# Second attention: stacks of single heads in half the partitions

## The chip, the cores and the metric

One core of one Trainium2 chip runs the whole program. The metric is the device time of one execution in microseconds (us); the median of several runs counts. TensorE (PE) multiplies, VectorE (DVE), ScalarE (ACT) and GpSimd (POOL) work on what it leaves, and SyncE (SP) issues nearly all transfers.

## What is computed

A two-layer network in float32 over 2 x 512 tokens of width 512. Each layer is attention and a feed-forward part, each followed by a residual sum and a layer norm. The change lies in the second attention: 32 query heads of 16 columns, 8 key/value heads, so that four query heads share one key head, causal.

```python
B, T, D_IN, D_OUT = (2, 256, 512, 512)
N_HEADS, N_KV = (32, 8)
HEAD_DIM = D_OUT // N_HEADS
...
q = _apply_rope(q, cos, sin)
k = _apply_rope(k, cos, sin)
k_h = jnp.repeat(k, GROUP_SIZE, axis=1)
v_h = jnp.repeat(v, GROUP_SIZE, axis=1)
scores = jnp.einsum('bhqd,bhkd->bhqk', q, k_h) / math.sqrt(HEAD_DIM)
causal = jnp.triu(jnp.ones((t, t), dtype=bool), k=1)
scores = jnp.where(causal[None, None], jnp.finfo(scores.dtype).min, scores)
attn = jax.nn.softmax(scores, axis=-1)
ctx = jnp.einsum('bhqk,bhkd->bhqd', attn, v_h)
```

(The sizes in the first line are not used: the arrays passed in have T = 512.)

## The kernel before

The program runs first attention, first feed-forward, second attention and second feed-forward one after another, each engine with an instruction list written out by hand. Products use a split of each float32 operand in a high and a low part (`fp32r`): `three` at L92 adds high x high, high x low and low x high.

In the second attention (`attention1`, L1253) a *unit* u is one key head of one batch (16 units), with four query heads; a *slot* s is one query head (64 slots). A head has only 16 columns, so the three terms of the split don't need three products: they are laid one under another in the partitions and one product sums over all. These layouts are the *stacks*. Before the change a stack holds a pair of heads: `q_stack` has the rows [q_hi; q_hi; q_lo] of two heads (3 x 32 = 96 partitions) for two pairs, and `k_stack` has two versions of [k_hi; k_lo; k_hi], each with the rows of the other head left at zero. Four stacks of each kind go round (`STACKS`, L1217). Turned queries and keys lie in `qT_hi`, `qT_lo`, `kT_hi`, `kT_lo`, and SP copies their rows into the stacks by transfers within the on-chip memory.

A slot does this. `scores` (L1911) computes the scores with queries in the partitions, four tiles of rows in three PSUM banks; VectorE takes each row's maximum (`maxima`, L1709). This runs seven slots ahead (`LEAD`). Once the four heads of a unit are through, PE turns the maxima (`turn_tops`, L1947), ScalarE copies them negated (`copy_tops`, L1514), and SP writes them as further rows of the query stack (`load_tops`, L1456), where the key stack has ones. `key_scores` (L1932) then computes the scores again, keys in the partitions and the maximum already taken off (98 rows), ScalarE takes exponentials (`exps`, L1506), GpSimd clears the masked triangles (`prune`), and `apply` (L1960) multiplies by the values, four heads at once in four column tiles of the array; from slot 5 on, three slots of four carry one of its three parts (L1978). `turn_output` (L1985) turns a unit's output, in the first slot of a unit.

The order of PE's slot, scores of s + 7 and keys of s alternating by bank (L2079):

```python
for s in range(SLOTS1):
    for piece in range(PIECES):
        if s + LEAD < SLOTS1:
            scores(s + LEAD, piece)
        key_scores(s, piece)
    if s % GROUP1 == 1 and s + 3 < SLOTS1:
        turn_tops((s + 3) // GROUP1)
```

SP's order, in one queue: stacks of units 0 and 1, then for every unit u the maxima of u (waiting for `top_ready`), then the stacks of u + 2 (waiting for `keyed` of unit u - 2, whose buffers they take). The score products of unit u + 2 start in slot 4u + 1 and wait for `stack_in`.

GpSimd prepares the key stacks (`pad_keys`, L1625: a fill with zeros and a select that writes the ones) between its additions for the rotation.

Of the kernel before, what the change touches and what calls it, by code (L numbers as in the profile page):

```python
# [10 lines left out]
F32 = mybir.dt.float32  # L11
# [4 lines left out]
P = 128  # L16
# [1177 lines left out]
PARTS = 3  # L1194
PAIR_ROWS = 2 * HD1
STACK = PARTS * PAIR_ROWS
# [19 lines left out]
STACK_DMAS = 16 * (2 * PARTS + 2 * PARTS)  # L1216
STACKS = 4  # L1217
TOP_ROW = STACK
STACK_ROWS = STACK + 2
# [33 lines left out]
def attention1(nc, t, w_o, w_f1, lora_b_in, small_in, result, psum):  # L1253

    ctx = ExitStack()
    with ctx:
# [17 lines left out]
        q_stack = [sb(f"q_stack{n}", [P, 2, SEQ], F32R) for n in range(2)]  # L1274
        k_stack = [sb(f"k_stack{n}", [P, 2, SEQ], F32R) for n in range(2)]
# [19 lines left out]
        q_stack.append(sb("q_stack2", [P, 2, SEQ], F32R))  # L1295
        k_stack.append(sb("k_stack2", [P, 2, SEQ], F32R))
# [6 lines left out]
        q_stack.append(over("q_stack3", [P, 2, SEQ], b_at, F32R))  # L1303
# [16 lines left out]
        low_at = aligned(nc.sbuf_base)  # L1320
        low = sb("low", [P, TILES, LORA])
        k_stack.append(over("k_stack3", [P, 2, SEQ], low_at, F32R))
# [51 lines left out]
        first_stack_in = sem("first_stack_in")  # L1374
        stack_in = [sem(f"stack_in{n}") for n in range(2)]
# [40 lines left out]

        def top_column(s, qt):
            u, h = divmod(s, GROUP1)
            at = (h % 2) * 2 * SEQ_TILES + (h // 2) * SEQ_TILES + qt
            return tops[:, u % 2, at:at + 1]  # L1420
# [8 lines left out]
        def _(sp):  # L1429
# [4 lines left out]
            def load_keys(u, version, arrived):  # L1434
                b, g = divmod(u, KV1)
                for part, source in enumerate((kT_hi, kT_lo, kT_hi)):
                    to = part * PAIR_ROWS + version * HD1
                    sp.dma_start(k_stack[u % STACKS][to:to + HD1, version, :].bitcast(F32),  # L1438
                                 source[g * HD1:(g + 1) * HD1, b * SEQ:(b + 1) * SEQ].bitcast(F32)).then_inc(arrived, 16)

            def load_queries(u, pair, arrived):
                b, g = divmod(u, KV1)
                first = (g % 2) * GROUP_COLS + pair * PAIR_ROWS
                for part, source in enumerate((qT_hi, qT_hi, qT_lo)):
                    sp.dma_start(q_stack[u % STACKS][part * PAIR_ROWS:(part + 1) * PAIR_ROWS, pair, :].bitcast(F32),  # L1445
                                 source[first:first + PAIR_ROWS, g // 2, b * SEQ:(b + 1) * SEQ].bitcast(F32)).then_inc(arrived, 16)

            def load_stacks(u):
                for n in range(2):
                    arrived = first_stack_in if u == 0 and n == 0 else stack_in[u % 2]  # L1450
                    load_keys(u, n, arrived)
                    load_queries(u, n, arrived)
# [3 lines left out]
            def load_tops(u):  # L1456
                sp.wait_ge(top_ready, u + 1)
                for version in range(2):
                    rows_of = slice(version * 2 * SEQ_TILES, (version + 1) * 2 * SEQ_TILES)
                    to = q_stack[u % STACKS][TOP_ROW + version:TOP_ROW + version + 1, :, :].rearrange("a p (t c) -> a (p t) c", c=P)  # L1460
                    sp.dma_start(to.bitcast(F32), top_rows[rows_of, :].bitcast(F32)).then_inc(top_in[u % 2], 16)  # L1461

            sp.wait_ge(stack_set, 2 * STACKS)
            sp.wait_ge(part_lo, TURNS_OF[0])
            load_stacks(0)
            load_stacks(1)
            for u in range(UNITS1):
                load_tops(u)
                if u + 2 < UNITS1:
                    if u + 2 == KV1:  # L1470
                        sp.wait_ge(part_lo, TURNS_OF[1])
                    if u >= 2:
                        sp.wait_ge(keyed, PIECES * GROUP1 * (u - 1))
                    load_stacks(u + 2)
# [140 lines left out]
        def _(pool):  # L1615
# [9 lines left out]
            def pad_keys(n):  # L1625

                pool.memset(k_stack[n][:, :, :].bitcast(F32), 0.0).then_inc(stack_set, 1)
                pool.wait_ge(stack_set, 2 * n + 1)
                pool.affine_select(k_stack[n][:, :, :], k_stack[n][:, :, :], [[-1, 2], [0, SEQ]], ALU.not_equal, 1.0,
                                   base=-TOP_ROW, channel_multiplier=1).then_inc(stack_set, 1)  # L1630

# [5 lines left out]
            for tile in range(TILES - 1):  # L1637
                turn_rows(tile)
                if tile < STACKS:
                    pad_keys(tile)  # L1640
# [251 lines left out]
        def _(pe):  # L1892
# [18 lines left out]
            def scores(s, piece):  # L1911

                u, h = divmod(s, GROUP1)
                tiles = SCORE_PIECES[piece]
                if piece == 0:
                    if s == 0:
                        pe.wait_ge(first_stack_in, STACK_DMAS // 2)
                    elif s == 1:
                        pe.wait_ge(stack_in[0], STACK_DMAS // 2)
                    elif h == 0:  # L1920
                        pe.wait_ge(stack_in[u % 2], (u // 2 + 1) * STACK_DMAS - (STACK_DMAS // 2 if u % 2 == 0 else 0))
# [10 lines left out]
            def key_scores(s, piece):  # L1932

                u, h = divmod(s, GROUP1)
                if h == 0 and piece == 0:
                    pe.wait_ge(top_in[u % 2], 32 * (u // 2 + 1))
# [283 lines left out]
```

## Time and profile before

| | us |
|---|---|
| median of 3 runs | 1212.97 (1212.17 to 1213.89) |
| profiled execution | 1218.12 |
| its span, first to last instruction | 1216.3 |
| mean granted TensorE clock | 0.959 |
| second attention, turns of units 0 to 15 | about 915 to 1136 |

The page gives each engine's busy time, the span in 40 slices with busy tenths and the granted clock, the transfers, the chain of work that ended last, and the costliest groups of instructions. In the views below a line is: start, duration (us), engine, line of the program, operation and tiles; in square brackets, how long the engine was idle before and what ended it. A granted clock of 1.00 is 2.4 GHz, 0.50 is 1.2 GHz. Names that begin with `a_` or `f_` are tiles of the second attention or laid over them; both occur for the four query stacks.

### The profile page before, as it was taken

The page shows a single profiled execution, that of the slowest core. Times are in us where ns is not written, and L with a number is a line of the kernel's source. Part 1 is how long each engine was busy: PE and PEld are TensorE (multiplying, and loading weights), DVE is VectorE, ACT ScalarE, POOL GpSimd, SP SyncE. Part 2 cuts the span into 40 slices and gives each one's busy share as a digit, 9 for nine tenths or more (in the row PEclk, how much of TensorE's full clock was granted, in tenths as well). Part 3 has the DMA queues.
Part 4 walks back from the last instruction along what each step waited for, and adds up shares of the span by engine and source line. Part 5 has one row for each costly group of instructions (what it writes and reads, how often), then busy time and mean ns, then how long its engine had stood idle before and what let it go on. Part 6 is the DMA issues. An engine that isn't in the chain of part 4 may idle for free. (4 is left out here: it accounts for less than half of the span.)

```text
span 1216.3 us, 19482 instructions
## 1 busy us (share of the span) xinstructions
PE 1146.2 (94%) x6266; PEld 947.1 (78%) x6266; DVE 736.9 (61%) x2384; ACT 638.7 (53%) x1486; POOL 464.2 (38%) x477
## 2 busy tenths in 40 slices
PE   7999999999999999999999999999997788779997
PEld 5888888888888888888888788888885555545786
DVE  6767776577766667766777622223367555655585
ACT  6656765566665666656655454531013444444624
POOL 4645553455544455444443243340152232232300
PEclk9999999999999999999999999999995878886999
DMA  6011110111100111101000022220012212320001
GB/s 223 18 44 36 35 36 27 37 28 28 51 26 12 44 36 36 39 24 36 27 27 1 19 78 76 71 80 1 18 30 50 58 40 50 107 47 21 2 1 70
DMA packets 30871, 51.30 MB, mean 42 GB/s; under 512 B 5936, under 2 KB 7088, under 8 KB 30768
## 3 DMA queue, kind: packets, MB, share of 16 engines
q1 hardware_dynamic: 30192, 48.99, 13.8%
q8 instruction: 52, 0.85, 0.3%
q10 hardware_dynamic: 576, 1.05, 0.2%
q14 instruction: 51, 0.42, 0.1%
HBM read 38.35 MB, written 2.10 MB: 33 GB/s over the span
## 5 line engine op out<-in xcount | busy, mean ns | idle before, releaser
L487 POOL TENSOR_TENSOR turned<-turned,sin 128x512 f32<-128x512 f32 x73 | 94.4, 1293 | 309.7 <-ACT turned L347 309.7
L1715 DVE CUSTOM_DVE_ANT_0 a_unused<-bank,a_mask 128x512 bf16<-128x512 f32 (+3 forms) x256 | 113.2, 488 | 86.9 <-PE bank L1926 85.3
L363 ACT ACTIVATE probs<-probs,neg_max 128x256 f32<-128x256 f32 (+1 forms) x256 | 119.8, 473 | 11.4 <-DVE neg_max L580 11.4
L1511 ACT ACTIVATE f_pT<-bank 128x512 f32<-128x512 f32 x144 | 67.6, 531 | 77.9 <-PE bank L1941 76.7
L490 POOL TENSOR_TENSOR turned<-turned,by_cos 128x512 f32<-128x512 f32 x73 | 101.0, 1384 | 5.7
L96 PE MATMUL bank<-wo_hi,oT_hi 128*128 128x512 f32 x256 | 100.3, 392 | 1.7 <-DVE oT_lo L643 1.7
L734 PE MATMUL bank<-xT_hi,wq_hi 128*128 128x512 f32 x256 | 101.5, 396 | 0.0
L734 PE MATMUL bank<-xT_lo,wq_hi 128*128 128x512 f32 x256 | 100.2, 391 | 0.0
L734 PE MATMUL bank<-xT_hi,wq_lo 128*128 128x512 f32 x256 | 100.0, 391 | 0.0
L96 PE MATMUL bank<-wo_hi,oT_lo 128*128 128x512 f32 x256 | 99.9, 390 | 0.0
L96 PE MATMUL bank<-wo_lo,oT_hi 128*128 128x512 f32 x256 | 99.7, 390 | 0.0
L1926 PE MATMUL bank<-a_k_stack,a_q_stack 96*128 96x512 f32 x192 | 69.6, 418 | 29.9 <-DMA a_q_stack<-a_qT_lo 26.5
L1926 PEld LDWEIGHTS bank<-a_k_stack,a_q_stack 96*128 96x128 f32 x192 | 45.2, 240 | 61.4 <-DMA a_q_stack<-a_qT_lo 29.5
L422 ACT ACTIVATE pT_hi<-bank 128x512 fp32r<-128x512 f32 x112 | 61.6, 595 | 52.4 <-PE bank L773 52.4
L426 ACT ACTIVATE oT_hi<-bank 128x512 fp32r<-128x512 f32 x64 | 38.2, 596 | 92.8 <-PE bank L96 92.8
L638 DVE TENSOR_TENSOR pT_lo<-bank,pT_hi 128x512 fp32r<-128x512 f32 x112 | 72.8, 686 | 21.5 <-ACT pT_hi L422 16.5
L576 DVE CUSTOM_DVE_ANT_0 probs<-bank,mask 128x256 f32<-128x256 f32 (+1 forms) x256 | 85.0, 386 | 0.0
L1659 POOL TENSOR_SCALAR_AFFINE_SELECT f_pT<-f_pT 128x256 f32<-128x256 f32 x96 | 36.7, 406 | 117.1 <-ACT f_pT L1511 117.1
L553 DVE TENSOR_TENSOR by_cos<-bank,cos 128x512 f32<-128x512 f32 x73 | 50.3, 689 | 49.4 <-ACT turned L347 49.3
L346 ACT ACTIVATE turned<-bank 64x512 f32<-64x512 f32 x73 | 43.5, 596 | 63.4 <-PE bank L734 62.8
L762 PE MATMUL bank<-kT_hi,qT_hi 128*128 128x256 f32 (+1 forms) x256 | 76.6, 299 | 0.0
L643 DVE TENSOR_TENSOR oT_lo<-bank,oT_hi 128x512 fp32r<-128x512 f32 x64 | 44.2, 691 | 48.9 <-ACT oT_hi L426 47.7
(248 smaller groups left out, 3296.5 us busy)
## 6 DMA issues: line engine op xcount, KB each, us to landing
staged<-weights SPq DMA_DIRECT2D x70, 256.0 KB, 2.7
f_staged<-weights_f SPq DMA_DIRECT2D x33, 256.0 KB, 2.7
a_q_stack<-a_qT_hi SPq DMA_DIRECT2D x48, 64.0 KB, 2.0
rows<-x_rows SPq DMA_DIRECT2D x2, 1024.0 KB, 7.4
out<-rows SPq DMA_DIRECT2D x8, 256.0 KB, 2.0
a_raw<-weights_qkv SPq DMA_DIRECT2D x4, 384.0 KB, 4.7
a_k_stack<-a_kT_hi SPq DMA_DIRECT2D x48, 32.0 KB, 2.0
a_q_stack<-a_qT_lo SPq DMA_DIRECT2D x24, 64.0 KB, 2.0
```

The lines of the kernel that those rows point to most:

```text
L96: mm = pe.matmul(out, a, b, start=(n == 0), stop=(n == len(steps) - 1))
L363: act.activation(probs[:, s % 2, h, 0:width], probs[:, s % 2, h, 0:width], ACT.Exp, bias=neg_max[:, s % 2, h:h + 1], scale=SCALE0, accum_o ...
L422: act.activation(pT_hi[:, kb, :], ps_t[kb][:, :], ACT.Copy).then_inc(pT_hi_done, 1)
L487: pool.tensor_tensor(at, at, sin[:, :], ALU.mult).then_inc(sin_done, 1)
L490: pool.tensor_tensor(at, at, by_cos_at(a, first), ALU.add).then_inc(roped, 1)
L576: dve.tensor_tensor_reduce(probs[:, s % 2, h, 0:width], ps_s[h // 2][:, (h % 2) * 2 * P:(h % 2) * 2 * P + width], seen, 1.0, LOWEST, ALU.a ...
L638: dve.tensor_tensor(pT_lo[:, kb, :], ps_t[kb][:, :], pT_hi[:, kb, :].bitcast(F32), ALU.subtract).then_inc(pT_lo_done, 1)
L734: mm = pe.matmul(ps_a[a % 2][:, :], w[hi][:, k, :], part[:, k, cols], start=(n == 0), stop=(n == 3 * KC - 1))
L762: mm = pe.matmul(ps_s[pair][:, (h % 2) * 2 * P:((h % 2) * 2 + count) * P], q[:, u % 2, h, at], k[:, u % 2, keys], start=(n == 0), stop=(n ...
L1511: act.activation(pT(s)[:, piece * SEQ:piece * SEQ + width], ps_t[piece][:, 0:width], ACT.Exp, scale=SCALE1).then_inc(exp_done, 1)
L1715: dve.tensor_tensor_reduce(unused[:, UNUSED_AT[qt]:UNUSED_AT[qt] + seen], ps_s[bank][:, at:at + seen], mask[:, SEQ - seen:SEQ], 1.0, LOWES ...
L1926: mm = pe.matmul(ps_s[piece][:, at:at + (qt + 1) * P], q_stack[u % STACKS][0:STACK, h // 2, qt * P:(qt + 1) * P], k_stack[u % STACKS][0:ST ...
```

## The change

A stack now holds single heads: 3 x 16 = 48 rows, and a 49th with the maxima against a row of ones. `q_stack` has the four heads of a unit side by side, `k_stack` one version. Two buffers of each exist, and each is used by halves: units alternate between partitions 0 to 48 and 64 to 112, so four units fit. The products name their place in the array (`tile_position`). A unit's stacks are six transfers (keys 32 KB, queries 128 KB each) and its maxima are one. SP issues the stacks of u + 2 ahead of the maxima of u. The key stacks are filled with ones, without a select. So that the four heads of a unit lie at the same partitions, the columns of the query weights are reordered on the host (a layout).

```diff
-PAIR_ROWS = 2 * HD1
-STACK = PARTS * PAIR_ROWS
+STACK = PARTS * HD1
+HALF_ROWS = P // 2
...
-STACK_DMAS = 16 * (2 * PARTS + 2 * PARTS)
+STACK_DMAS = 16 * (PARTS + PARTS)
 STACKS = 4
+STACKS_AHEAD = 2
 TOP_ROW = STACK
-STACK_ROWS = STACK + 2
+STACK_ROWS = STACK + 1
...
-        q_stack = [sb(f"q_stack{n}", [P, 2, SEQ], F32R) for n in range(2)]
-        k_stack = [sb(f"k_stack{n}", [P, 2, SEQ], F32R) for n in range(2)]
+        q_stack = [sb(f"q_stack{n}", [P, GROUP1, SEQ], F32R) for n in range(STACKS // 2)]
...
+        k_stack = [sb(f"k_stack{n}", [P, SEQ], F32R) for n in range(STACKS // 2)]
...
+        def stack_of(u):
+
+            buffer, upper = u // 2 % 2, u % 2
+            return q_stack[buffer], k_stack[buffer], upper * HALF_ROWS
...
-            def load_keys(u, version, arrived):
+            def load_stacks(u):
                 b, g = divmod(u, KV1)
-                for part, source in enumerate((kT_hi, kT_lo, kT_hi)):
-                    to = part * PAIR_ROWS + version * HD1
-                    sp.dma_start(k_stack[u % STACKS][to:to + HD1, version, :].bitcast(F32),
-                                 source[g * HD1:(g + 1) * HD1, b * SEQ:(b + 1) * SEQ].bitcast(F32)).then_inc(arrived, 16)
-
-            def load_queries(u, pair, arrived):
-                b, g = divmod(u, KV1)
-                first = (g % 2) * GROUP_COLS + pair * PAIR_ROWS
-                for part, source in enumerate((qT_hi, qT_hi, qT_lo)):
-                    sp.dma_start(q_stack[u % STACKS][part * PAIR_ROWS:(part + 1) * PAIR_ROWS, pair, :].bitcast(F32),
-                                 source[first:first + PAIR_ROWS, g // 2, b * SEQ:(b + 1) * SEQ].bitcast(F32)).then_inc(arrived, 16)
-
-            def load_stacks(u):
-                for n in range(2):
-                    arrived = first_stack_in if u == 0 and n == 0 else stack_in[u % 2]
-                    load_keys(u, n, arrived)
-                    load_queries(u, n, arrived)
+                queries, keys, base = stack_of(u)
+                of, cols = slice(g * HD1, (g + 1) * HD1), slice(b * SEQ, (b + 1) * SEQ)
+                arrived = stack_in[u % 3]
+                for part, (q_part, k_part) in enumerate(((qT_hi, kT_hi), (qT_hi, kT_lo), (qT_lo, kT_hi))):
+                    to = slice(base + part * HD1, base + (part + 1) * HD1)
+                    sp.dma_start(keys[to, :].bitcast(F32), k_part[of, cols].bitcast(F32)).then_inc(arrived, 16)
+                    sp.dma_start(queries[to, :, :].bitcast(F32), q_part[of, :, cols].bitcast(F32)).then_inc(arrived, 16)
 
             weights_out(0)
             weights_out(1)
             def load_tops(u):
                 sp.wait_ge(top_ready, u + 1)
-                for version in range(2):
-                    rows_of = slice(version * 2 * SEQ_TILES, (version + 1) * 2 * SEQ_TILES)
-                    to = q_stack[u % STACKS][TOP_ROW + version:TOP_ROW + version + 1, :, :].rearrange("a p (t c) -> a (p t) c", c=P)
-                    sp.dma_start(to.bitcast(F32), top_rows[rows_of, :].bitcast(F32)).then_inc(top_in[u % 2], 16)
-
-            sp.wait_ge(stack_set, 2 * STACKS)
+                queries, _, base = stack_of(u)
+                to = queries[base + TOP_ROW:base + TOP_ROW + 1, :, :].rearrange("a p (t c) -> a (p t) c", c=P)
+                sp.dma_start(to.bitcast(F32), top_rows[0:GROUP1 * SEQ_TILES, :].bitcast(F32)).then_inc(top_in[u % 2], 16)
+
+            sp.wait_ge(stack_set, STACKS // 2)
             sp.wait_ge(part_lo, TURNS_OF[0])
-            load_stacks(0)
-            load_stacks(1)
+            for u in range(STACKS_AHEAD):
+                load_stacks(u)
             for u in range(UNITS1):
+                ahead_of = u + STACKS_AHEAD
+                if ahead_of < UNITS1:
+                    if ahead_of == KV1:
+                        sp.wait_ge(part_lo, TURNS_OF[1])
+                    if ahead_of >= STACKS:
+                        sp.wait_ge(keyed, PIECES * GROUP1 * (ahead_of - STACKS + 1))
+                    load_stacks(ahead_of)
                 load_tops(u)
-                if u + 2 < UNITS1:
-                    if u + 2 == KV1:
-                        sp.wait_ge(part_lo, TURNS_OF[1])
-                    if u >= 2:
-                        sp.wait_ge(keyed, PIECES * GROUP1 * (u - 1))
-                    load_stacks(u + 2)
                 if u == 3:
...
             def pad_keys(n):
-
-                pool.memset(k_stack[n][:, :, :].bitcast(F32), 0.0).then_inc(stack_set, 1)
-                pool.wait_ge(stack_set, 2 * n + 1)
-                pool.affine_select(k_stack[n][:, :, :], k_stack[n][:, :, :], [[-1, 2], [0, SEQ]], ALU.not_equal, 1.0,
-                                   base=-TOP_ROW, channel_multiplier=1).then_inc(stack_set, 1)
+                pool.memset(k_stack[n][:, :].bitcast(F32), 1.0).then_inc(stack_set, 1)

...
                 tiles = SCORE_PIECES[piece]
+                queries, keys, base = stack_of(u)
                 if piece == 0:
-                    if s == 0:
-                        pe.wait_ge(first_stack_in, STACK_DMAS // 2)
-                    elif s == 1:
-                        pe.wait_ge(stack_in[0], STACK_DMAS // 2)
-                    elif h == 0:
-                        pe.wait_ge(stack_in[u % 2], (u // 2 + 1) * STACK_DMAS - (STACK_DMAS // 2 if u % 2 == 0 else 0))
+                    if h == 0:
+                        pe.wait_ge(stack_in[u % 3], (u // 3 + 1) * STACK_DMAS)
                 if s >= 1:
                     pe.wait_ge(max_done, SEQ_TILES * (s - 1) + maxima_before(tiles[-1]))
                 for qt in tiles:
                     at = SCORES_AT[qt][1]
                     mm = pe.matmul(ps_s[piece][:, at:at + (qt + 1) * P],
-                                   q_stack[u % STACKS][0:STACK, h // 2, qt * P:(qt + 1) * P],
-                                   k_stack[u % STACKS][0:STACK, h % 2, 0:(qt + 1) * P], start=True, stop=True,
-                                   skip_group_check=True)
+                                   queries[base:base + STACK, h, qt * P:(qt + 1) * P],
+                                   keys[base:base + STACK, 0:(qt + 1) * P], start=True, stop=True,
+                                   skip_group_check=True, tile_position=(base, 0))
                 mm.then_inc(scored, 1)
 
             def key_scores(s, piece):
 
                 u, h = divmod(s, GROUP1)
+                queries, keys, base = stack_of(u)
                 if h == 0 and piece == 0:
-                    pe.wait_ge(top_in[u % 2], 32 * (u // 2 + 1))
+                    pe.wait_ge(top_in[u % 2], 16 * (u // 2 + 1))
                 if s >= 1:
                     pe.wait_ge(exp_done, PIECES * (s - 1) + piece + 1)
                 for kb in KEY_PIECES[piece]:
                     at = KEYS_AT[kb][1]
                     mm = pe.matmul(ps_t[piece][:, at:at + SEQ - kb * P],
-                                   k_stack[u % STACKS][0:STACK_ROWS, h % 2, kb * P:(kb + 1) * P],
-                                   q_stack[u % STACKS][0:STACK_ROWS, h // 2, kb * P:SEQ], start=True, stop=True,
-                                   skip_group_check=True)
+                                   keys[base:base + STACK_ROWS, kb * P:(kb + 1) * P],
+                                   queries[base:base + STACK_ROWS, h, kb * P:SEQ], start=True, stop=True,
+                                   skip_group_check=True, tile_position=(base, 0))
                 mm.then_inc(keyed, 1)
...
-    qkv = np.concatenate([inputs["L1_attn_Wq"], inputs["L1_attn_Wk"], inputs["L1_attn_Wv"]], 1)
+    by_place = inputs["L1_attn_Wq"].reshape(D, KV1, GROUP1, HD1).transpose(0, 2, 1, 3).reshape(D, D)
+    qkv = np.concatenate([by_place, inputs["L1_attn_Wk"], inputs["L1_attn_Wv"]], 1)
```

## Rows read from the trace of the kernel before

**Rows 1.** The page: TensorE and the other engines' busy time, and its clock by slices
```profile
PE 1146.2 (94%) x6266; PEld 947.1 (78%) x6266; DVE 736.9 (61%) x2384; ACT 638.7 (53%) x1486; POOL 464.2 (38%) x477
...
PEclk9999999999999999999999999999995878886999
```

**Rows 2.** The chain that ended last, in order of time: start, us, what; 1091 to 1106
```profile
1091.35 2.03 DMA a_q_stack<-a_qT_lo
...
1096.74 0.68 SPq L1461
...
1105.09 2.67 DMA f_q_stack<-a_qT_lo
```

**Rows 3.** Instructions of the SP queue in order of time
```profile
919.09 1.45 SPq L1461 DMA_DIRECT2D a_q_stack<-f_top_rows  x2
...
968.46 1.08 SPq L1432 DMA_DIRECT2D a_staged<-weights_o  x2
...
1110.14 1.38 SPq L1461 DMA_DIRECT2D a_q_stack<-f_top_rows  x2
```

**Rows 4.** Waits, 925 to 1110 us: us in total, times, longest
```profile
PE bank L1926 <- DMA a_q_stack<-a_qT_lo: 26.5, 9, 4.3
...
PE bank L1926 <- DMA f_q_stack<-a_qT_lo: 12.0, 4, 3.8
PEld bank L1978 <- issue: 4.4, 15, 1.1
```

**Rows 5.** Transfers by line: count, size of each, median us from issue to landing
```profile
a_q_stack<-a_qT_lo SPq DMA_DIRECT2D x24, 64.0 KB, 2.0
a_staged<-weights_o SPq DMA_DIRECT2D x4, 256.0 KB, 3.0
```

**Rows 6.** VectorE in order of time: first maximum of a head and end of its last
```profile
1072.05 0.69 DVE L1715 CUSTOM_DVE_ANT_0 a_unused<-bank,a_mask 128x512 bf16<-128x512 f32 x1 [2.59 <-PE bank L1926]
...
1073.72 0.08 DVE L1715 DVE_READ_ACCUMULATOR2_ANT f_tops<- 128x1 f32 x1
```

**Rows 7.** TensorE in order of time, starts of slots at clock 1.00
```profile
983.57 0.50 PE L1926 MATMUL bank<-a_k_stack,a_q_stack 96*128 96x512 f32 x1
...
985.33 0.48 PE L1926 MATMUL bank<-a_k_stack,a_q_stack 96*128 96x512 f32 x1
...
992.42 0.50 PE L1926 MATMUL bank<-a_k_stack,a_q_stack 96*128 96x512 f32 x1
```

**Rows 8.** The same view, slots at clock 0.50
```profile
929.53 0.80 PE L1926 MATMUL bank<-a_k_stack,a_q_stack 96*128 96x512 f32 x1 [2.18 <-DMA a_q_stack<-a_qT_lo]
...
943.26 0.80 PE L1926 MATMUL bank<-f_k_stack,f_q_stack 96*128 96x512 f32 x1 [3.76 <-DMA f_q_stack<-a_qT_lo]
...
946.12 1.94 PE L1978 MATMUL bank<-f_pT,a_v_tok 128*32 128x512 f32 x8
947.99 0.80 PE L1926 MATMUL bank<-f_k_stack,f_q_stack 96*128 96x512 f32 x1
...
1110.92 0.80 PE L1926 MATMUL bank<-f_k_stack,f_q_stack 96*128 96x512 f32 x1
...
1119.09 0.80 PE L1926 MATMUL bank<-f_k_stack,f_q_stack 96*128 96x512 f32 x1
...
1121.61 1.05 PE L1988 MATMUL bank<-identity,a_oT_now 128*128 128x128 f32 x4
```

**Rows 9.** The same view, an idle time of TensorE as the stage starts
```profile
914.72 0.49 PE L1926 MATMUL bank<-a_k_stack,a_q_stack 96*128 96x512 f32 x1 [1.87 <-DVE f_tops L1715]
```

**Rows 10.** Stretches: us, TensorE busy (instructions), granted clock, DMA share, GB/s
```profile
48.90:51.60 2.70, 2.70 (x15) 0.50 0.42 118
51.70:55.00 3.30, 3.30 (x22) 1.00 0.01 3
929.50:939.30 9.80, 9.77 (x33) 0.50 0.14 33
943.30:949.30 6.00, 6.00 (x20) 0.50 0.02 4
949.40:954.50 5.10, 5.10 (x46) 1.00 0.31 72
...
1110.00:1123.40 13.40, 13.40 (x64) 0.50 0.00 1
```

More of the change, by code:

```diff
@@ L1294, in attention1 @@
         o_tok = q_tok
-        q_stack.append(sb("q_stack2", [P, 2, SEQ], F32R))
-        k_stack.append(sb("k_stack2", [P, 2, SEQ], F32R))
+        k_stack = [sb(f"k_stack{n}", [P, SEQ], F32R) for n in range(STACKS // 2)]
         unused = sb("unused", [P, HEAD_PROBS], BF16)
@@ L1302, in attention1 @@
         sb("b_place", [P, 2, D])
-        q_stack.append(over("q_stack3", [P, 2, SEQ], b_at, F32R))
         oT_now = sb("oT_now", [P, SEQ])
@@ L1319, in attention1 @@
         small = sb("small", [P, sum(SMALL.values())])
-        low_at = aligned(nc.sbuf_base)
         low = sb("low", [P, TILES, LORA])
-        k_stack.append(over("k_stack3", [P, 2, SEQ], low_at, F32R))
         h_at = aligned(nc.sbuf_base)
@@ L1373, in attention1 @@
         part_ready, part_hi, part_lo = sem("part_ready"), sem("part_hi"), sem("part_lo")
-        first_stack_in = sem("first_stack_in")
-        stack_in = [sem(f"stack_in{n}") for n in range(2)]
+        stack_in = [sem(f"stack_in{n}") for n in range(3)]
         scored, max_done = sem("scored"), sem("max_done")
@@ L1415, in pT @@
             return pT_in_x[:, n, :] if n < RING_IN_X else pT_rest[:, n - RING_IN_X, :]
+        def stack_of(u):
+            buffer, upper = u // 2 % 2, u % 2
+            return q_stack[buffer], k_stack[buffer], upper * HALF_ROWS
         def top_column(s, qt):
             u, h = divmod(s, GROUP1)
-            at = (h % 2) * 2 * SEQ_TILES + (h // 2) * SEQ_TILES + qt
+            at = h * SEQ_TILES + qt
             return tops[:, u % 2, at:at + 1]
@@ L1638, in _ @@
                 turn_rows(tile)
-                if tile < STACKS:
+                if tile < STACKS // 2:
                     pad_keys(tile)
```

## The prediction, made before the changed kernel was run

> **What bounds the kernel now.** I read the page first [rows 1]: TensorE (PE) is busy 94% of the span, but in slices 31 to 36 of 40, the second attention, its figures fall to 7 and 8 and the granted clock to 5 to 8 tenths. This is the only stretch where the page shows room. Then the chain of waits inside that stretch [rows 2]. The reader is to see one pattern that repeats: a transfer lands in a query stack, the product of L1926 runs, an exponential of L1511 ends, and then nothing but transfers being issued by SP until the next stack lands. The queue itself [rows 3] shows why: a group of heads ("unit" below, four heads) costs SP 14 issues: two rows of maxima (L1461), then twelve for the stacks of the unit after next. The first of one unit starts at 1096.74 and the last at 1105.09 us [rows 2], 13 steps in 8.35, so 0.64 us each. The first rows of maxima go out at 919.09 us, the fifteenth at 1110.14: 14 periods of 13.65 us. 14 issues of 0.64 are 9.0 of these; the rest is the landing (2.0 us), the first product, the exponentials and the turned maxima, in series, because the twelve issues stand behind the wait for maxima on the same queue. PE stood idle for it 38.5 us (26.5 + 12.0) from 925 to 1110 us [rows 4].
>
> The idling costs a second time. TensorE's granted clock is 5 to 8 tenths there [rows 1], since it falls to 1.2 GHz (0.50) at most of these waits, and part of the next unit is computed at that level. So there are two questions: how long a unit is when no stack is late, and at which of the two clock levels it runs.
>
> **The change part by part.**
>
> *Queue.* A unit costs 7 issues in place of 14: 7 x 0.64 = 4.5 us, and the six for unit u+2 now stand ahead of the maxima of unit u. They wait only for `keyed` of unit u-2. From there to the turned maxima of u lie the rest of one slot (a slot is one head in PE's loop), a slot of 1.76 us, over half of one of 2.57 [rows 7] and ScalarE's copy: an estimate of 5 us at the fast clock, against 6 x 0.64 = 3.8 us of issuing, so the maxima are not held up. Behind SP's new wait are queued the maxima of u and, in units 3, 8 and 9, the weights; if it ran short, the maxima still have two slots before PE needs them. The query transfers grow to 128 KB over 16 partitions, four pieces a row. No row shows this shape: 64 KB lands in 2.0 us and 256 KB from HBM in 3.0 [rows 5]. I take 2.4; both ends cost nothing, since a stack is first read six slots after its issue. Two issues of 256 KB take SP 1.08 [rows 3], so a larger transfer costs it no more. The stack wait goes, all 38.5 us of it.
>
> *GpSimd.* Four fills and four selects become two fills of half the width. GpSimd is busy 38% of the span [rows 1] and in neither chain row; worth 0, and it can't cost.
>
> *What is late next.* With no stack wait PE's own order sets the pace. VectorE needs 1.75 us a head (the four maxima, 1072.05 to 1073.80) [rows 6], 7.0 a unit, and a join of less than one. PE, at 2.4 GHz, has one unit in the trace in which no stack was late [rows 7]: its slots start at 983.57, 985.33 and, three later, 992.42, so 1.76 + 7.09 (2.57 + 2.26 + 2.26) = 8.85 us. At 1.2 GHz [rows 8]: the slot with maxima and first apply part 4.73 (943.26 to 947.99), the next two 8.17 (1110.92 to 1119.09), the slot with the turned output 3.57 (1119.09 to 1121.61 + 1.05), together 16.47 us. The old period, 13.65, lies between. Everything hangs on the clock.
>
> *The products.* Each score and key product has the same columns as before but sums over 48 or 49 rows in place of 96 or 98. Columns set its time, so I take the same length. Every product now stands in one half of the array.
>
> *The clock.* It falls at about 915 us, after PE idles 1.87 us for the maxima while the stage starts [rows 9]. The change doesn't touch this wait, so it falls again. What brings it back? Take four stretches [rows 10]. From 48.9 to 51.6 us PE runs products over all 128 rows, and the clock is back at once. From 929.5 to 939.3 us it runs score and key products over 96 and 98 rows, 9.77 of 9.80 us busy, at 0.50 throughout: the clock doesn't return. From 943.3 the first apply part follows, 1.94 us on the whole array [rows 8], and from 949.4 the clock is back; six of the eight returns of the stage come within about 2 us of such a part's end. From 1110.0 to 1123.4 us PE is busy all the time, later apply parts included, and stays at 0.50 for 13 us. So back-to-back work over 96 rows is not enough, with apply parts mixed in it is just enough or just not. The change takes half the rows out of exactly these products and leaves the applies as they are. On this reading the mixture falls short everywhere, and the stage stays at 1.2 GHz from 915 us until the scores end. No row shows 48-row products, so it is an inference; the bounds are "never back" and "back as before".
> The Trainium skill (page "TensorE: Matmul & The Clock Gate", section "Loop structure matters more than you think") says that matmuls kept back to back keep the clock up and waits for DMA bring it down. It speaks of no rows. By it the change repairs the clock. The stretch at 929.5 us is against that rule as a full account.
>
> *Sum at 1.2 GHz* (profiled execution: 1218.12 us, span 1216.3). Slot 1 starts at 929.53 after a wait of 2.18 [rows 8], so now at 927.4. Slots 1 to 4 take 9.8 (929.5 to 939.3 [rows 10]), to 937.2; slots 5 to 7 take 4.73 + 8.17, to 950.1. Twelve units of 16.47 bring slot 56 to 1147.7, and it ends at 1151.3, against 1122.7 before: +28.6. In one slot of four (the first of a unit) scores are of unit u+1 and keys of unit u, in different halves, and can overlap. Column tiles of the apply do so in the trace (eight products of 512 columns in 1.94 us, where one of full width takes 0.80 [rows 8]); row halves aren't shown. Overlap can bring the 2.35 us of scores and keys (9.8 / 4, less the turn) down to VectorE's 1.75: 13 x 0.6 = 7.8 us less; I take it, with 0 as the other end. The first slots after 1122.7 (keys, apply, turns) are also slow until the clock returns: an apply part of 1.94 has about half of it to lose and the keys about half a us, 1.4 a slot for one or two: +2. Together +22.8: 1240.9. The median of the runs lies 5.15 under the profiled execution: 1235.8, so 1236.
>
> *Changes of tiling.* PE's loads sat 0.29 us (4.4 us, 15 times) at a change from full-array work to the apply tiles [rows 4]. Now the score and key products are tiled too, so turning the maxima adds one such change a unit and turning the output two. Bounds: 0, and 3 x 0.29 x 13 = 11 us. I take 0, since at 1.2 GHz the known changes lie inside the measured slots, and keep 11 for the range.
> The Trainium skill (page "TensorEngine Tiling (Array Packing)", section "Key Properties") says that a change of mode drains the engine, while tiles of one mode run in parallel. It gives no price; the row's 0.29 us is the only one here.
>
> **The rivals.**
> *Clock as before (faster).* If 48 rows count like 96, the first apply, slot 5, brings the clock back and nothing takes it down again, since no wait of over 2 us is left. Slot 5 ends at 941.9; slots 6 and 7 take 5.2 (an estimate between 2 x 2.26 and 8.17, near the first, since the clock comes back in slot 6 in the trace), to 947.1; twelve units of 8.85 and 1.76 end slot 56 at 1055.1: 67.6 us less, 1150.5, or 1145 as a median; with up to 11 us of tiling changes 1156. I take 1148. For it: six returns of the clock came with a first apply part, which is unchanged. Against it: the stretch of 9.8 us. It decides from the point where one return occurs between 937 and 1000 us; the skill's rule above gives this result.
> *Clock returns late or in part.* Returns depend on how an apply part falls, as the 13 us from 1110 show. One return half way would give half of each: (1236 + 1148) / 2 = 1192.
> *No overlap, and every change of tiling paid.* 1236 + 8 + 11 = 1255, the clock staying down.
>
> **How the numbers follow.** Clock stays down 0.62 (own range 1222 to 1252); as before 0.24 (1143 to 1158); in part 0.10 (1160 to 1220); all costs paid 0.04. The likeliest gives 1236. Signs, with 0.2% (2.4 us) as what a measurement can tell: slower 0.60, within 0.05, faster 0.35. The range must reach into the fast case: 1146 to 1252 holds about 0.85.
>
> **What would show it.** In the changed trace: the PE waits for a stack transfer gone; the maxima rows issued at the unit's period, 16 us (this forecast) or 9 (rival); the granted clock 0.50 from 915 to past 1120 us, or 1.00 from about 942; score and key products overlapping once in four slots. The forecast is wrong if the clock returns while score products are still running. If slots at 0.50 are much shorter than 4.08 us, the overlap is larger than I took; if longer, the tiling is dearer.

## The result, and the profile after

The changed kernel takes 1190.82 us (median of four runs: 1161.81, 1176.65, 1204.98, 1209.67) against 1212.57 (1211.55 to 1213.89) of the kernel before. The ratio is 0.9642 (0.9536 to 0.9748) without the two runs in which the clock was low for longest, and 0.982 by the medians of all. Each of the four is below the fastest run of the kernel before. The spread is part of the result, and its cause is the subject of what follows. The forecast was slower, 1236. The profiled execution is the one of 1204.98 us, with a span of 1203.3.

The page of the changed kernel: TensorE's busy time, its clock in 40 slices of the span, the DMA issues of the stacks (KB each, us to landing).

```profile
span 1203.3 us, 19359 instructions
PE 1171.3 (97%) x6266; PEld 954.1 (79%) x6266; DVE 737.5 (61%) x2384; ACT 641.0 (53%) x1486; POOL 457.4 (38%) x471
...
PEclk9999999999999999999999999999997555598899
...
a_q_stack<-a_qT_hi SPq DMA_DIRECT2D x32, 128.0 KB, 3.3
...
a_q_stack<-a_qT_lo SPq DMA_DIRECT2D x16, 128.0 KB, 3.8
```

TensorE (PE) is busy 97% of the span in place of 94 [rows 1], and busy 25 us longer with the same 6266 products in a span 13 us shorter: it waits less and computes more slowly. The clock reads 5 in slices 32 to 35, where it had read 8, 7, 8 and 8 [rows 1].

TensorE in three stretches of the changed kernel, with the columns of [rows 10].

```profile
918.60:1048.10 129.50, 128.80 (x552) 0.50 0.32 44
1048.30:1102.70 54.40, 53.79 (x424) 1.00 0.43 64
1102.90:1119.80 16.90, 16.90 (x76) 0.50 0.01 1
```

This is the picture. From 918.6 us TensorE is busy 128.8 of 129.5 us at 1.2 GHz (granted clock 0.50). Before, no stretch of this stage at 0.50 was longer than 34.1 us (915.2 to 949.3). Then the clock is back for 54 us, and low again for 17 us near the end of the stage.

The waits of the same stage, 915 to 1123 us (us in total, times, longest).

```profile
PEld bank L1909 <- issue: 29.9, 36, 1.7
...
PEld bank L1909 <- DVE f_tops L1701: 17.1, 30, 1.9
```

No wait for a stack is left in this window; those of [rows 4] were 38.5 us. Ahead of it TensorE is idle for 1.54 us before its first score product, which the profile puts down to the first stack; the product starts at 907.7 in place of 905.5 us. What remains is on the weight loads, which run beside the products. The queue of SP shows the new order (start us, us, what): the six issues of a unit stand 0.6 us apart and come before the maxima.

```profile
982.17 0.52 SPq L1441 DMA_DIRECT2D a_k_stack<-a_kT_hi  x1
982.74 0.63 SPq L1442 DMA_DIRECT2D a_q_stack<-a_qT_hi  x1
...
989.47 0.55 SPq L1450 DMA_DIRECT2D a_q_stack<-f_top_rows  x1
```

TensorE in order of time: first a unit at 0.50, by the first score product of each slot, then one at 1.00.

```profile
954.85 0.79 PE L1909 MATMUL bank<-a_k_stack,a_q_stack 48*128 48x512 f32 x1
...
959.76 0.79 PE L1909 MATMUL bank<-a_k_stack,a_q_stack 48*128 48x512 f32 x1
...
967.92 0.79 PE L1909 MATMUL bank<-a_k_stack,a_q_stack 48*128 48x512 f32 x1
...
970.43 0.80 PE L1909 MATMUL bank<-a_k_stack,a_q_stack 48*128 48x512 f32 x1
```

```profile
1056.96 0.49 PE L1909 MATMUL bank<-a_k_stack,a_q_stack 48*128 48x512 f32 x1
...
1065.72 0.49 PE L1909 MATMUL bank<-a_k_stack,a_q_stack 48*128 48x512 f32 x1
```

A slow unit is 4.91 + 8.16 (two slots) + 2.51 = 15.58 us, a fast one 8.76. Each unit that the stage stays at 1.2 GHz costs 6.8 us. The short slot, 2.51 us, is the one in which scores and keys lie in different halves of the partitions; they start together and take 1.47 us (1045.87 to 1047.34, below).

TensorE as the clock returns.

```profile
1044.43 1.51 PE L1962 MATMUL bank<-f_pT,a_v_tok 128*32 128x128 f32 x16
1045.87 0.79 PE L1909 MATMUL bank<-a_k_stack,a_q_stack 48*128 48x512 f32 x1
1045.87 0.79 PE L1925 MATMUL bank<-a_q_stack,a_k_stack 49*128 49x512 f32 x1
...
1047.34 1.04 PE L1972 MATMUL bank<-identity,a_oT_now 128*128 128x128 f32 x4
1048.31 0.50 PE L1909 MATMUL bank<-a_k_stack,a_q_stack 48*128 48x512 f32 x1
```

The products take 0.79 us up to here and 0.50 from here. The return stands right behind a third apply part, an overlapped slot and the turned output (L1972), in one row. The same three had stood at the ends of the six units before it (the turned output at 953.80 us and every 15.59 us from there), and hadn't brought the clock back.

### The profile page after: what moved, and what is told of

It reads as the page before. It is cut to its first block and busy times, and to the rows that moved or that the text cites. A ratio compares the mean times of both kernels' runs of the same rounds, so it can differ in the third digit from the quotient of the medians.

```text
span 1203.3 us, 19359 instructions
## 1 busy us (share of the span) xinstructions
PE 1171.3 (97%) x6266; PEld 954.1 (79%) x6266; DVE 737.5 (61%) x2384; ACT 641.0 (53%) x1486; POOL 457.4 (38%) x471
## 5 line engine op out<-in xcount | busy, mean ns | idle before, releaser
L1909 PEld LDWEIGHTS bank<-a_k_stack,a_q_stack 48*128 48x128 f32 x256 | 64.0, 261 | 56.6 <-issue 32.0
L1909 PE MATMUL bank<-a_k_stack,a_q_stack 48*128 48x512 f32 (+3 forms) x256 | 96.9, 454 | 4.0 <-DVE f_tops L1701 2.4
L1925 PE MATMUL bank<-a_q_stack,a_k_stack 49*128 49x512 f32 (+3 forms) x256 | 90.7, 432 | 0.0
```

What stands on the lines that cost most here:

```text
L1909: mm = pe.matmul(ps_s[piece][:, at:at + (qt + 1) * P], queries[base:base + STACK, h, qt * P:(qt + 1) * P], keys[base:base + STACK, 0:(qt + ...
L1925: mm = pe.matmul(ps_t[piece][:, at:at + SEQ - kb * P], keys[base:base + STACK_ROWS, kb * P:(kb + 1) * P], queries[base:base + STACK_ROWS, ...
```

## The experiments

Two theories. ROWS: whether the clock returns depends on how many rows of the array the products span; the change removes the queue's wait (a gain) and halves the rows (a loss). RIVAL: rows don't matter; what the clock does here comes from tiling, from the waits or from chance. Lines and numbers below are those of each kernel's own profile. The kernel before, run beside them, took 1213.9, 1213.77 and 1213.53 us in the three batches.

**The kernel before, its products over half the rows.** The key products are cut in the same way as the scores shown.

```diff
-                                   q_stack[u % STACKS][0:STACK, h // 2, qt * P:(qt + 1) * P],
-                                   k_stack[u % STACKS][0:STACK, h % 2, 0:(qt + 1) * P], start=True, stop=True,
+                                   q_stack[u % STACKS][0:STACK // 2, h // 2, qt * P:(qt + 1) * P],
+                                   k_stack[u % STACKS][0:STACK // 2, h % 2, 0:(qt + 1) * P], start=True, stop=True,
...
```

> The kernel before with one edit: its score and key products sum over the first 48 rows of the stacks in place of 96 and 98 (so half of each sum and the maxima are left out; columns, count and order of all instructions are the same). Theory ROWS (the fewer rows these products span, the harder TensorE's clock comes back from 1.2 GHz): the clock stays at 0.50 through most of the stage, a unit takes about 16.5 us of TensorE instead of 13.65, and the time is about 1250 us (1235 to 1258). Rival GAPS (only waits of TensorE set the clock, rows do not): the same returns as before, 1212 us within 2.

Measured: 1270.05 us (1266.36 to 1270.33), ratio 1.0461 (1.0427 to 1.0495). Stretch, and a unit of its TensorE:

```profile
916.60:1189.50 272.90, 266.32 (x1082) 0.50 0.17 41
```

```profile
999.68 0.79 PE L1926 MATMUL bank<-a_k_stack,a_q_stack 48*128 48x512 f32 x1
...
1016.44 0.79 PE L1926 MATMUL bank<-f_k_stack,f_q_stack 48*128 48x512 f32 x1
```

The kernel before loses the clock for 273 us, all of the stage, by nothing but the number of rows. Queue, order, transfers and columns are those of before. A unit takes 16.76 us (999.68 to 1016.44), and of stack waits 6.0 us are left of 38.5, since TensorE is now slower than the queue. This is the state that the prediction forecast for the changed kernel, and it exists. It was 20 us dearer than expected, outside the range given. The rival falls in its part "rows don't matter", and tiling can't be the reason here, since this kernel gives these products no place in the array.

**The order of issue alone, on the kernel before.** Arrivals are counted by three semaphores in place of two, as in the change.

```diff
-                load_tops(u)
                 if u + 2 < UNITS1:
                     ...
                     load_stacks(u + 2)
+                load_tops(u)
...
```

> The kernel before with one part of the change alone: the stacks of unit u+2 are issued ahead of the maxima of unit u (and a third arrival semaphore for the stacks). Still 14 transfers a unit, 96 and 98 rows. ROWS: the clock comes back with the first apply part, before 950 us, and stays, since no stack is waited for; a unit is then the larger of TensorE's 8.85 us and SP's 14 x 0.64 = 9.0, so about 9.3: 1155 us (1148 to 1167), and the runs agree within 3 us. GAPS: the same mean, but returns that scatter as in the changed kernel, runs apart by tens of us.

Measured: 1160.43 us (1159.99 to 1165.12), ratio 0.9578 (0.9543 to 0.9613). Stretches, and what is left of waits:

```profile
916.00:943.10 27.10, 25.86 (x91) 0.50 0.28 65
943.30:1100.00 156.70, 148.81 (x1124) 1.00 0.24 59
```

```profile
PE bank L1941 <- DMA a_q_stack<-f_top_rows: 5.2, 5, 2.0
```

With all 14 issues and 96 rows, the order alone gains 53 us, more than the whole change, and runs alike each time. The stack waits go, and with them what took the clock down: it returns at 943.2 us and stays. The twelve issues ahead of the maxima leave waits for the turned maxima, the 5.2 us of this line and 1.7 under the name f_q_stack, which the changed kernel with its six doesn't have.

**Seven transfers, but the old order.**

```diff
+                load_tops(u)
                 ahead_of = u + STACKS_AHEAD
                 ...
                     load_stacks(ahead_of)
-                load_tops(u)
```

> The changed kernel with SP's old order: the maxima of unit u first, then the six transfers of the stacks of u+2. The other part of the change alone. The serial chain of a unit loses 7 of its 14 issues: 13.65 - 7 x 0.64 = 9.2 us, below a slow unit (15.6) and 0.4 above a fast one (8.8). So the order adds nothing to seven transfers: the changed kernel's scatter, 1162 to 1215 us, with stack waits under 0.5 us a unit. If the order were needed, stack waits of 2 us or more a unit return and the time is over 1200 in every run.

Measured: 1232.57 us (1224.5 to 1237.3), ratio 1.0154 (1.0094 to 1.0214): missed. I had expected the scatter of the changed kernel; it is slower than both. Stretches, and TensorE at the second one's end:

```profile
917.20:1033.00 115.80, 112.67 (x482) 0.50 0.32 40
1033.20:1046.70 13.50, 11.21 (x88) 1.00 0.50 97
1046.90:1135.40 88.50, 88.50 (x400) 0.50 0.28 42
```

```profile
1044.32 0.50 PE L1909 MATMUL bank<-a_k_stack,a_q_stack 48*128 48x512 f32 x1 [2.29 <-DMA a_q_stack<-a_qT_lo]
```

At 1.2 GHz the unit is longer than the queue's period, and after 940 us no stack is late (two were before, by 0.80 and 1.74 us). As soon as the clock is back the unit is shorter than that, a stack comes 2.29 us late, and the clock is gone for another 88 us. The chain of waits there has a transfer of 4.78 us from SP's issue to its landing:

```profile
1038.85 0.59 SPq L1441
...
1039.49 4.78 DMA a_q_stack<-a_qT_lo
```

The 9.2 us that I had expected of the queue kept the landing of 2.0 us of before; this one is 2.8 us longer, and SP's issues of maxima around it lie 11.0 us apart (1035.65 and 1046.67), more than a fast unit of 8.8. The sign named for the other case, stack waits of 2 us or more a unit, didn't come either: there are three, of 4.8 us together, since TensorE is slow for nearly the whole stage.

So halving the issues isn't enough: the order is what keeps a regained clock. The order alone gains 53 us; the transfers, the halves and the 48 rows without it lose 19.

**Sixteen products more, over 128 rows and over 48.** Both add work to the changed kernel, once, ahead of the first apply part. The second has `qT_hi[0:48, ...]` where the first has `qT_hi[0:128, ...]`.

```diff
+                if u == 0 and part == 0:
+                    for n in range(16):
+                        pe.matmul(ps_o[0][:, :], qT_hi[0:128, 0, 0:P], qT_hi[0:128, 0, 0:SEQ], start=True, stop=True,
+                                  skip_group_check=True)
```

> The changed kernel with 16 products more, 512 columns over all 128 rows, into the bank that the first apply part overwrites, ahead of it (slot 5). They cost 16 x 0.43 = 7 us at 1.2 GHz. ROWS: they bring the clock back at about 945 us and it stays to the end of the scores: about 1154 us (1147 to 1162), runs within 5 us of each other. GAPS: no effect on the clock, so the changed kernel's scatter (1162 to 1210) plus 7 us.

> The same 16 products as in the run with 128 rows, same columns and place, but over 48 rows. ROWS: they do not bring the clock back, so the changed kernel's scatter plus 7 us, 1165 to 1217 us. Rival BURST (any burst back to back does it): the same as with 128 rows, about 1154 us.

Measured over 128 rows: 1154.74 us (1154.5 to 1155.97), ratio 0.9524 (0.9496 to 0.9552). Over 48 rows: 1189.62 (1169.62, 1189.2, 1190.04, 1216.29). The products and the stretches, first 128 rows, then 48:

```profile
939.48 6.45 PE L1959 MATMUL bank<-a_qT_hi 128*128 128x512 f32 x16
...
939.50:945.00 5.50, 5.50 (x14) 0.50 0.40 44
945.10:1090.00 144.90, 144.29 (x1117) 1.00 0.38 56
```

```profile
940.76 7.19 PE L1959 MATMUL bank<-a_qT_hi 48*128 48x512 f32 x16
...
939.50:946.00 6.50, 6.50 (x17) 0.50 0.47 52
946.10:1022.40 76.30, 76.30 (x340) 0.50 0.27 37
1022.60:1100.00 77.40, 76.79 (x608) 1.00 0.44 69
```

The two kernels differ in one number. The same sixteen products, in the same place, of the same columns and back to back, give the clock back while they run (at 945.1 us) over 128 rows and do nothing over 48. With 128 rows the kernel is also steady: the scatter of 48 us is gone, so it came from the time of the return. This settles ROWS for the return of the clock. It also gives an estimate of what the change is worth when the clock comes back there: 1154.74 less the 6.45 us of the sixteen products is 1148.3, and the late return costs the changed kernel the other 42 us.

**Halves by pairs of units.** The score products run seven slots ahead of the key products, so in three slots of four they belong to units u+2 and u. If halves alternate by pairs, these three slots have scores and keys in different halves, where the change has them so in one slot of four.

```diff
-            buffer, upper = u // 2 % 2, u % 2
+            buffer, upper = u % 2, u // 2 % 2
```

> The changed kernel with one line changed: buffer u % 2 and half u // 2 % 2, so that the scores of unit u+2 and the keys of unit u, which share three slots of four, lie in different halves of the array. OVERLAP with ROWS: score and key products overlap in three or four slots of four (1.47 us in place of 2.35 at 1.2 GHz); the array is then as full as with 96 rows, the clock comes back with one of the first apply parts, before 960 us, in every run; slots fall to VectorE's 1.75 to 2.2 us, a unit to about 7.9: 1134 us (1126 to 1147), runs within 6 us. If overlap alone matters and rows do not bring the clock back: a return scattered as in the changed kernel, 1140 to 1190.

Measured: 1135.85 us (1135.37 to 1138.9), ratio 0.9371 (0.9336 to 0.9407). Stretches, and a unit:

```profile
918.70:942.40 23.70, 23.07 (x94) 0.50 0.37 43
942.60:1080.00 137.40, 134.72 (x1155) 1.00 0.40 59
```

```profile
985.42 0.49 PE L1909 MATMUL bank<-a_k_stack,a_q_stack 48*128 48x512 f32 x1
...
993.33 0.50 PE L1909 MATMUL bank<-a_k_stack,a_q_stack 48*128 48x512 f32 x1
```

Products of both halves together span 97 rows, and the clock returns at 942.5 us, as it did over 96 and 98 rows. A unit is 7.91 us in place of 8.76: the overlap is also worth something at the full clock, over thirteen units 11 of the 12 us between 1148.3 and 1135.9. Run again with nothing changed, it took 1138.35 (1134.58 to 1148.04), ratio 0.9378 (0.9353 to 0.9404):

> Halves by pairs once more, on the same chip as the changed kernel: 1136 us, runs within 5 us; now and then one with a loss of the clock in the middle (up to 1152).

The profiled execution was the one of 1148.04, and shows why. From the last score product to the end of the program it takes 107.4 us, where the first profile of this version takes 95.2: 12.2 of the 12.6 us between the two spans.

```profile
1030.00:1041.00 11.00, 10.54 (x90) 1.00 0.01 3
1041.10:1068.40 27.30, 27.30 (x119) 0.50 0.00 1
```

The clock fell at 1041.1 us, after a stretch in which no wait of TensorE or of its loads was over 1.7 us. With the 128-row products added to it this version was no better:

> The same with the 16 full-row products of the earlier run ahead of the first apply part. If the clock came back by itself in the run without them, they cost up to 7 us: 1140 us; if not, they fix it: about 1136 us, runs within 3 us.

Measured 1145.13 us (1139.65 to 1151.6), ratio 0.9425 (0.9368 to 0.9481), with a fall of the same kind from 1044.7 to 1072.0 us in the profiled execution, of 1151.6. The two lower runs, 1139.65 and 1139.88, fit the 1140 of the clock coming back by itself.

**Key products over 64 rows.** The rest of the half is filled with zeros, so the key products sum over 64 rows in place of 49, scores still over 48. SP also waits for the two further fills; the first score product starts no later for it (907.3 against 907.7 us).

```diff
+                pool.memset(q_stack[n][:, :, :].bitcast(F32), 0.0).then_inc(stack_set, 1)
...
-                                   keys[base:base + STACK_ROWS, kb * P:(kb + 1) * P],
-                                   queries[base:base + STACK_ROWS, h, kb * P:SEQ], start=True, stop=True,
+                                   keys[base:base + HALF_ROWS, kb * P:(kb + 1) * P],
+                                   queries[base:base + HALF_ROWS, h, kb * P:SEQ], start=True, stop=True,
```

> The changed kernel with its key products over 64 rows in place of 49 (the query stacks are filled with zeros first, so the further rows add nothing). Columns unchanged. ROWS: a little more of the array is used and the clock comes back earlier on average: median 1150 to 1185 us, still scattered. GAPS: as the changed kernel, median about 1190.

Measured: 1155.67 us (1153.86 to 1174.63), ratio 0.9526 (0.9483 to 0.957). In its profiled execution, of 1153.86, the clock returns at 952.2:

```profile
918.00:952.00 34.00, 33.37 (x133) 0.50 0.31 37
952.20:1080.00 127.80, 127.19 (x1000) 1.00 0.42 62
```

Fifteen more rows in half of these products, filled with zeros, bring the return forward, though one run (1174.63, mean granted clock 0.964 against 0.981 to 0.983 in the others) still had it late. Both together, pairs and 64 rows:

> Halves by pairs together with key products over 64 rows. Columns, slots and waits as with halves by pairs alone. ROWS: the clock comes back no later and holds with more to spare; 1136 us (1133 to 1140), and the loss of the clock that the burst variant showed in some runs does not occur. If the further rows cost time (filling the query stacks with zeros on GpSimd, 2 x about 2 us while the stage starts), 1 to 3 us more.

Measured: 1135.65 us in five runs from 1133.98 to 1135.66, ratio 0.9355 (0.9341 to 0.9369). This beats both kernels, by 78 and 52 us (against 1213.53 and 1187.99 beside it), and its runs lie within 1.7 us.

```profile
944.00:1100.00 156.00, 152.50 (x1260) 1.00 0.36 53
```

That it holds the clock in every execution rests on these five; of the ten runs of pairs without the zeros four took over 1138 us, so five could also be chance.

**The changed kernel once more**, in more rounds:

> The changed kernel once more, for its scatter: no mechanism is taken away. ROWS: the return of the clock falls at another unit in each run, each unit later costing 15.6 - 8.8 = 6.8 us; runs between about 1150 and 1215 us, median 1175 to 1195. If the scatter of the first runs was a disturbance of that chip, they now agree within 5 us.

Measured: 1187.99 us (1161.32, 1174.56, 1187.89, 1188.09, 1190.21, 1207.6). The profiled execution took 1174.56, with a span of 1172.8, and

```profile
918.90:998.90 80.00, 79.37 (x337) 0.50 0.32 41
999.10:1090.00 90.90, 90.29 (x706) 1.00 0.43 65
1090.00:1110.00 20.00, 20.00 (x144) 1.00 0.01 1
```

This checks the sum for the scatter. The return came 49.2 us earlier than in the first profile (999.1 against 1048.3), which is 49.2 / 15.6 = 3.2 slow units, each worth 6.8 us: 21.5. The second fall, 17 us at 0.50 from 1102.9, isn't there: at 15.6 to 8.8 that is 17 x (1 - 8.8 / 15.6) = 7.4. Together 28.9 of the 30.5 us between the spans. The profiles agree: the last score product starts 22.7 us earlier (1077.2 against 1099.9), and from there to the end it is 95.6 us in place of 103.4, 7.8 less. Between these two executions, when the clock returns is three quarters of the difference, and the second fall the rest.

## Why the prediction was wrong, point by point

**The sign.** The forecast "clock stays down" had 0.62, and what came is the case with 0.10, "returns late or in part", priced at 1192 and measured at 1190.8 and 1188.0. Its price was half way between the two others because I had no row to place the return; that it lay so near is luck. The sign given for being wrong came too: the clock returned at 1048.3 us, and score products ran until 1100.

**The step that failed** is one sentence: "the mixture falls short everywhere, and the stage stays at 1.2 GHz from 915 us until the scores end". The reading of rows under it was right. In the profiled execution 48-row products, with the apply parts between them, didn't bring the clock back in 130 us, the kernel before with 48 rows stays down for 273 us, and the two kernels with sixteen products show it by themselves. Wrong was "everywhere". The same prediction had counted, two paragraphs on, a slot in four where scores and keys overlap, and used it for time only. It is also the one kind of slot in which products of this stage span 97 rows together. In the five profiles with halves by single units and no 128-row products added (1048.3, 999.1, 1033.2, 1022.6 and, with 64 rows, 952.2 us) the return stands right behind such a slot and the turned output. In the kernel before with 48 rows, which has no halves and so no such slot, there is no return. That the overlap makes the return possible fits that contrast and the halves by pairs, but it isn't shown by itself: no run takes the overlap out of the changed kernel. Why it comes at one unit and not at the six before, no run shows.

The Trainium skill (page "TensorE: Matmul & The Clock Gate", section "Loop structure matters more than you think") says that products kept back to back keep the clock up. Taken as the whole rule it gave the time of the rival "clock as before", 1148. The row of 128.8 us busy in 129.5 at 0.50 shows that it isn't the whole rule here.

The price of that rival was right: the run with 128 rows, less its sixteen products, gives 1148.3. What failed is when the clock returns, not what a unit costs at either level.

**The queue.** The stack waits went, all 38.5 us, as forecast, and the maxima aren't held up. The issues are 0.57 to 0.67 us apart (0.64). But the prediction took queue and order as one term. The order by itself is worth 53 us; the rest of the change in the old order costs 19.

**The landing** was mis-sized: 3.3 and 3.8 us as medians, 4.78 at one place, where I took 2.4 from [rows 5]. The size of a transfer isn't all of it, since the key transfers kept their 32 KB and their 16 partitions and land later too, first before, then after:

```profile
a_k_stack<-a_kT_hi SPq DMA_DIRECT2D x48, 32.0 KB, 2.0
```

```profile
a_k_stack<-a_kT_hi SPq DMA_DIRECT2D x32, 32.0 KB, 3.1
```

With the new order alone they still land in 2.0 us, so it isn't the order; that they go out between larger query transfers is the difference left, and no run tests it. The longer landing costs nothing in the changed kernel from the second unit on, as forecast, since a stack is read six slots later; the idle 1.54 us before the stage's first product may be its price there, and in the old order it is part of a wait that took the clock.

**The units.** Fast unit: 8.85 forecast, 8.76 measured. Slow unit: 16.47 less 0.6 for the overlap is 15.87, measured 15.58. The overlap is larger: I let VectorE's 1.75 us a head be its floor, but scores and keys took 1.47 in place of 2.35, and VectorE still has the whole slot, 2.51 us, for its 1.75.

**Changes of tiling** were taken at 0 with a bound of 11 us. They don't show: both units are shorter than forecast without them, so 0 was right to within the 0.3 us a unit by which they are shorter.

**Not forecast at all**: the second fall of the clock, at 1102.8 us, worth 7 to 8 us in the profiled execution. I had written that with no wait of over 2 us left nothing takes it down. TensorE's longest idle time there is this:

```profile
1102.40 0.30 PE L1942 MATMUL bank<-identity,f_tops 128*128 128x128 f32 x1 [0.61 <-DVE a_q_tok L1712]
```

In three profiles (1102.8 here, 1041.1 and 1044.7 in the versions with pairs) it fell without such a wait, each time in the first slots after the scores have ended, at the turned maxima that follow key products alone. The second profile of the changed kernel has the same place and no fall, so the place doesn't suffice.

**The range**, 1146 to 1252, reached to the fast case and held every run of the changed kernel. The chance of 0.6 for slower was too high, because cases between the two levels, where both mechanisms act in turn, had been given 0.10. Given one row where the mixture was "just enough or just not" [rows 8, 10], a return at some unit among thirteen deserved more than that.

## What to carry to other kernels

Before halving the rows of a product to save transfers, ask which clock level the stage will run at: a kernel that gains 53 us from the order of its queue gave back 30 of them, on balance, with products over 48 rows in place of 96. If rows must be halved, place what is in flight together in different halves; here one line turned 1190 us, scattered over 48, into 1136 (1134.6 to 1148.0 in ten runs). And when a queue is the bound, reorder it before making its transfers fewer.

## What the runs showed of the hardware

- TensorE's clock, once at 1.2 GHz, stayed there through 130 us (changed kernel) and 273 us (kernel before, 48 rows) of nearly unbroken products over 48 and 49 rows. Sixteen 512-column products over 128 rows brought it back within 5.6 us; the same sixteen over 48 rows, 7.2 us of them, did not.
- Rows filled with zeros count: key products over 64 rows in place of 49 moved the median from 1190 to 1156 us.
- The same program returned to 2.4 GHz at different places in different executions (999.1 and 1048.3 us), which made 1161 to 1210 us of it. Here a scatter of some per cent on one core was mostly a clock that returned late.
- The clock can also fall with no long wait: at 1041.1 us after 11.0 us of which TensorE was busy 10.5. All three such falls lie just after the last score products, a place that other executions pass at 2.4 GHz; what takes it down there stays open.
- Products in different halves of the partitions run side by side: scores and keys of a head took 1.47 us in place of 2.35 at 1.2 GHz.
- A transfer of 128 KB into 16 partitions landed in 3.3 to 3.8 us (medians), where one of 64 KB had landed in 2.0 [rows 5]; 32 KB transfers issued between them took 3.1 in place of 2.0.
